# Scaling h by 1/z on VectorE behind the reciprocal, instead of on GpSimd

## The reference

```
h  = x @ W;  f1 = h @ a1;  f2 = h @ a2
e  = leaky_relu(f1 + f2^T, 0.2)
att = softmax(adj * e, axis=1)            # each column of the 2048x2048 scores sums to one
xp = att @ h + bias + x                   # layer 0
y  = adj @ (xp @ W1 + b1)                 # layer 1
y  = relu((y - mean) * rsqrt(var + 1e-5) * gamma + beta)   # statistics over all batches and nodes
out = y + xp
```

## Time and profile before

| | |
|---|---|
| three runs | 1035.03, 1036.02, 1036.68 us; median 1036.02 |
| profiled execution, first to last instruction | 1034.5 us (the runs' times also hold what lies around that: median minus span is 1.5 us) |
| VectorE busy | 937.6 us, 91% |
| TensorE busy | 943.3 us, 91% (ends of matmuls are modelled) |
| ScalarE busy | 771.1 us, 75% |
| GpSimd busy | 553.1 us, 53% |
| batches 1 to 6 | 119.5 to 123.6 us each, from one recip of tile 0 to the next |

### The profile page before, as it was taken

The page is one execution under the profiler, slowest core; times in us unless marked ns, Lnnn a source line. Parts: engine busy times, 40 slices in busy tenths (PEclk is TensorE's granted clock), DMA queues, the critical chain, the costliest instruction groups (busy, mean ns, idle before and its releaser), DMA issues.

```text
span 1034.5 us, 11295 instructions
## 1 busy us (share of the span) xinstructions
PE 943.3 (91%) x2999; PEld 529.0 (51%) x2999; DVE 937.6 (91%) x938; ACT 771.1 (75%) x897; POOL 553.1 (53%) x306
## 2 busy tenths in 40 slices
PE   7998999979999799989999799997999989998980
PEld 5333555555555545546555545555555555554760
DVE  4987899998999699997999959998899979998967
ACT  5877688857887578785878657885788758787646
POOL 1434566664776356673667626665467636666000
PEclk8999999999999999999999999998999999999995
DMA  8955454565456454555445644455545555434978
GB/s 333 421 190 196 177 180 171 202 221 204 173 188 212 168 193 167 224 174 214 165 172 213 219 161 173 173 203 193 204 173 203 211 191 195 175 120 167 355 284 324
DMA packets 45153, 214.14 MB, mean 207 GB/s; under 512 B 5406, under 2 KB 6030, under 8 KB 23438
## 3 DMA queue, kind: packets, MB, share of 16 engines
q1 hardware_dynamic: 45084, 213.32, 56.1%
HBM read 189.07 MB, written 24.23 MB: 206 GB/s over the span
## 4 chain that ended last, share of the span: by engine, by line
issue 35%; DVE 30%; PE 13%; ACT 9%; POOL 7%; DMA 3%; DVEq 2%; ACTq 0%; SPq 0%; POOLq 0%
DVE exp_lo L685 14%; DVE scores L656 7%; DVE scores L666 6%; ACT scores L535 6%; POOL hz L811 3%; PE acc L392 2%; PE acc L430 2%; ACT scores L544 1%; PE acc L457 1%; PE acc L460 1%; PE acc L459 1%; POOL region_even L829 1%; POOL region_odd L829 1%; PE acc L422 1%; DMA f_odd<-biasT 1%
## 5 line engine op out<-in xcount | busy, mean ns | idle before, releaser
L666 DVE CUSTOM_DVE_ANT_0 scores<-scores,adj_slot 128x2048 f32<-128x2048 f32 x128 | 292.1, 2282 | 5.1 <-DVE scores L656 1.8
L544 ACT ACTIVATE scores<-scores,neg_mx 128x2048 f32<-128x2048 f32 x128 | 256.5, 2004 | 4.2
L811 POOL TENSOR_TENSOR hz<-region_even,rz 128x128 f32<-128x128 f32 x64 | 143.4, 2241 | 195.7 <-DVE rz L673 190.0
L811 POOL TENSOR_TENSOR hz<-region_odd,rz 128x128 f32<-128x128 f32 x64 | 140.1, 2190 | 182.5 <-DVE rz L673 178.7
L443 PE MATMUL acc<-adj_slot,region_even 128*128 128x512 f32 x512 | 230.8, 596 | 4.1 <-issue 4.1
L408 PE MATMUL acc<-scores,hz 128*128 128x512 f32 x464 | 209.3, 595 | 12.7 <-POOL hz L811 12.6
L685 DVE TENSOR_TENSOR exp_lo<-scores,exp_hi 128x512 fp32r<-128x512 f32 x280 | 215.6, 827 | 3.8 <-ACT exp_hi L554 3.8
L443 PE MATMUL acc<-adj_slot,region_odd 128*128 128x512 f32 x392 | 175.3, 592 | 0.8 <-DVE region_odd L717 0.8
L656 DVE SCALAR_TENSOR_TENSOR scores<-scores,f,f_even 128x2048 f32<-128x2048 f32 x64 | 156.8, 2450 | 12.3 <-ACT scores L535 12.1
L656 DVE SCALAR_TENSOR_TENSOR scores<-scores,f,f_odd 128x2048 f32<-128x2048 f32 x64 | 157.9, 2467 | 8.6 <-issue 6.5
L422 PE MATMUL acc<-exp_hi,hz_lo 128*128 128x512 f32 x280 | 132.2, 472 | 36.7 <-POOL hz_lo L823 36.1
(11 more groups left out here) (79 smaller groups left out, 847.6 us busy)
## 6 DMA issues: line engine op xcount, KB each, us to landing
adj_slot<-adjT SPq DMA_DIRECT2D x128, 1024.0 KB, 4.8
adj_slot<-xT SPq DMA_DIRECT2D x13, 1024.0 KB, 9.2
adj_slot<-xp_dram SPq DMA_DIRECT2D x8, 1024.0 KB, 7.0
adj_slot<-y_dram SPq DMA_DIRECT2D x7, 1024.0 KB, 7.0
outT<-adj_slot SPq DMA_DIRECT2D x6, 1024.0 KB, 4.7
f_odd<-f_rows SPq DMA_DIRECT2D x4, 1024.0 KB, 6.7
region_even<-xT SPq DMA_DIRECT2D x16, 256.0 KB, 4.9
f_even<-biasT SPq DMA_DIRECT2D x16, 256.0 KB, 4.1
```

Of the source, the lines that this page charges most:

```text
L544: act.activation(scores[e][:, :], scores[e][:, :], ACT.Exp, bias=neg_mx[:, e:e + 1], accum_out=zsum[:, e:e + 1]).then_inc(exp_done, 1)
L666: dve.tensor_tensor_reduce(scores[e][:, :], scores[e][:, :], slots[s][:, :], 1.0, NEG_BIG, ALU.mult, ALU.max, mx[:, e:e + 1]).then_inc(max ...
L811: scaled = pool.tensor_tensor(hz[e][:, :], region[bt.par][:, tile_cols(t)], rz[:, e:e + 1].to_broadcast([P, P]), ALU.mult)
```

## The change

VectorE now runs scale_h(t) directly behind recip(t), for all 128 tiles, with `tensor_scalar` (the scalar is rz) instead of GpSimd's `tensor_tensor` with a broadcast rz. For a split tile the two instructions that made hz and hz_hi on GpSimd become one that makes hz_hi, and hz_lo = h * rz - hz_hi is one `scalar_tensor_tensor`. VectorE gets the waits of scale_h (h_out, the ring, rz_done, split_used, hz_scaled) and loses wait_hz. GpSimd keeps only its four add_bias a batch.

```diff
             def recip(bt, t):
                 e = t % ER
                 dve.wait_ge(exp_done, NT * bt.n + t + 1)
-                wait_hz(bt, t)
                 dve.reciprocal(rz[:, e:e + 1], zsum[:, e:e + 1]).then_inc(rz_done, 1)
+            def scale_h(bt, t):
+                e = t % ER
+                if t % TC == 0:
+                    dve.wait_ge(h_out, NC * bt.n + t // TC + 1)
+                wait_ring(dve, bt, t)
+                dve.wait_ge(rz_done, NT * bt.n + t + 1)
+                if t in WHOLE or is_first(bt):
+                    dve.tensor_scalar(hz[e][:, :], region[bt.par][:, tile_cols(t)], rz[:, e:e + 1], None,
+                                      ALU.mult).then_inc(hz_done, 1)
+                    return
+                m = SPLIT.index(t)
+                dve.wait_ge(split_used, NS * bt.n + NC * (m - 1))
+                dve.tensor_scalar(hz_hi[m % 2][:, :], region[bt.par][:, tile_cols(t)], rz[:, e:e + 1], None,
+                                  ALU.mult).then_inc(hz_scaled, 1)
+                dve.wait_ge(hz_scaled, len(SPLIT) * (bt.n - 1) + m + 1)
+                dve.scalar_tensor_tensor(out=hz_lo[e][:, :], in0=region[bt.par][:, tile_cols(t)], scalar=rz[:, e:e + 1],
+                                         in1=hz_hi[m % 2][:, :].bitcast(F32), op0=ALU.mult, op1=ALU.subtract)\
+                    .then_inc(hz_done, 1)
...
                         recip(bt, t)
+                        scale_h(bt, t)
...
                 if not is_last(bt):
                     recip(nx, 0)
+                    scale_h(nx, 0)
...
         def _(pool):
-            def scale_h(bt, t):
-                e = t % ER
-                pool.wait_ge(rz_done, NT * bt.n + t + 1)
-                if t % TC == 0:
-                    pool.wait_ge(h_out, NC * bt.n + t // TC + 1)
-                wait_ring(pool, bt, t)
-                scaled = pool.tensor_tensor(hz[e][:, :], region[bt.par][:, tile_cols(t)],
-                                            rz[:, e:e + 1].to_broadcast([P, P]), ALU.mult)
-                if t in WHOLE or is_first(bt):
-                    scaled.then_inc(hz_done, 1)
-                    return
-                scaled.then_inc(hz_scaled, 1)
-                m = SPLIT.index(t)
-                pool.wait_ge(split_used, NS * bt.n + NC * (m - 1))
-                pool.tensor_tensor(hz_hi[m % 2][:, :], region[bt.par][:, tile_cols(t)],
-                                   rz[:, e:e + 1].to_broadcast([P, P]), ALU.mult).then_inc(hz_scaled, 1)
-                pool.wait_ge(hz_scaled, 2 * (len(SPLIT) * (bt.n - 1) + m + 1))
-                pool.tensor_tensor(hz_lo[e][:, :], hz[e][:, :], hz_hi[m % 2][:, :].bitcast(F32),
-                                   ALU.subtract).then_inc(hz_done, 1)
...
             def step(bt):
-                for t in range(NT):
-                    scale_h(bt, t)
-                    if t == NT - 2 and not is_first(bt):
-                        add_bias(bt, 0)
-                        add_bias(bt, 1)
-                for c in range(0 if is_first(bt) else 2, NC):
+                for c in range(NC):
                     add_bias(bt, c)
```

More of the change, by code:

```diff
@@ L671, in recip @@
                 dve.wait_ge(exp_done, NT * bt.n + t + 1)
-                wait_hz(bt, t)
                 dve.reciprocal(rz[:, e:e + 1], zsum[:, e:e + 1]).then_inc(rz_done, 1)
-            def wait_hz(bt, t):
-                if not (is_first(bt) and t < ER):
-                    dve.wait_ge(hz_done, NT * bt.n + t - ER + 1)
+            def scale_h(bt, t):
[16 more added lines that the diff above has]
+                    .then_inc(hz_done, 1)
             def exp_low(bt, t):
```

## The result

| | before | after |
|---|---|---|
| median of the runs, us | 1036.35 (1035.03 to 1036.85) | 1062.56 (1059.46 to 1063.69) |
| profiled execution: time, span | 1036.02, 1034.5 | 1059.46, 1057.7 |
| granted TensorE clock, profiled execution | 0.969 | 0.968 |

The changed kernel takes 1.0242 times as long, 95% interval 1.0219 to 1.0264: 26 us slower. The forecast was 3.9 us slower, with a range up to 1057 and a chance of 0.13 for the rival that comes nearest, exposed waits. The profiled execution of after is its fastest; the other three have spans of 1060.0 to 1061.9 at clocks of 0.960 to 0.965, and all that follows is read from spans of profiled executions.

A forecast was written before the change was run, and what follows sets the result against it. VectorE was taken to set the mid-batch pace, with TensorE waiting at batch ends. Stream +12.3, batch 0 +1.5 and ends -9.9 gave +3.9 us on a 1034.5 span: 1038.4, median 1040; range 1024 to 1057.

The forecast's parts named there:

- exposed waits: VectorE's rz_done and hz_scaled waits expose register work, 0.2 us more a split tile, 0.1 a whole one: 1057 us; chance 0.13.
- The port relief: Mid-batch, VectorE's exp_lo and leaky get shorter without GpSimd's products on the shared port: 5.35 us a batch saved.
- 0.034 us: On VectorE, an instruction waiting for its forerunner's semaphore starts this long after the forerunner's end.
- 0.045: Split tiles on VectorE: cost in us of the extra split_used wait before the product, taken from between 0 and 0.15.
- tensor_scalar's 0.23 us: VectorE's new 128x128 product, not in the trace, was priced as the nearest instruction, a copy of 128x128.
- The ends: Six batch ends: support product earlier as TensorE no longer waits for hz_lo; five gain 1.5 us, one 2.4, together 9.9.
- The other ends are like batch 3's: Batch ends other than batch 5's were taken to match batch 3's within 0.15 us, gaining 1.5 us each.
- done with tile 15 at about 469.5: End of batch 3: with hz there, TensorE finishes tile 15 then, before the first xp at 471.65 us.
- Batch 0: Whole tiles alone, 0.14 us each, 2.2 us, partly hidden by waits for the exponential: +1.5 us, between 0 and 3.5.
- TensorE's wait for hz_lo at the ends: Sign at batch ends: TensorE's 3.74 us wait for tile 15's hz_lo would be gone.

The follow-up runs named there:

- products later: Changed kernel, for tiles 1 to 14 the first product placed behind the next score and the second behind the leaky after it; 1025.43 us, 0.9885 of before.
- the run with the small instructions: Changed kernel with ten small VectorE instructions ahead of all other work, five kinds at 128 and 512 columns, each behind its forerunner's semaphore; one execution, 1059.11 us.
- the run with the waits ahead: Changed kernel with the waits on h_out, TensorE's ring and split_used moved before the reciprocal's own; 1050.01 us, 1.0126 of before.
- the kernel before with the adds held: Kernel before the change, GpSimd's adds of batches 1 to 7 waiting until exp_lo of tile 15 is through; 1013.98 us, 0.9788 of before.

## Why the prediction was wrong

**The bound and the direction were right.** VectorE paces the stream and what is added to it is paid in full; the change is slower. The port relief came as priced: with the measured 0.42 us a whole tile, 0.87 a split one behind an exp_low, 0.73 one without (0.95 less 0.22), tiles 0 to 13 add some 9.1 us a batch, and the streams grew by 27.5/7 = 3.9, which leaves 5.2 for the relief (5.35 forecast). The run with GpSimd's products put back prices them at 31.0/7 = 4.4, at other places.

**The step that failed is what a wait costs.** The forecast took "0.034 us" behind a forerunner and "0.045" for split_used, from a gap at the kernel's start where one wait had one direct forerunner. That made a gap behind the reciprocal of 0.034 us in a whole tile and 0.079 in a split one. Measured are 0.11 and 0.19; over the seven streams the gaps sum to 17.2 us instead of 6.2. What was missed is that a wait on another semaphore in front of the product keeps the queue from having the product ready when the reciprocal ends, even if its condition is long true. Moving such waits took 11.0 us out of the streams, of which the forecast held 63 x 0.045 = 2.8: 8.2 us missed. The rival "waits are exposed" had named this mechanism, but got 0.13, because I argued that a few queue instructions would run under the new instructions. They stand under a reciprocal of 0.16 us and not under one of 0.29, and under a whole score or leaky they cost nothing (products later). Nor is the price one number: in batch 7, outside the loop, where the same waits have constant values, seven of the nine split tiles have a gap of 0.09 us instead of 0.19. No run isolates why.

The Trainium skill, "VectorE: DVE Perf Modes", "The DRAIN you can't avoid", has semaphores between chained instructions cost nothing extra. The runs don't agree. Between small instructions with one direct semaphore each the gap is 0.03 us, while a leaky without such a wait starts 0.09 us before the end of the tensor_scalar in front of it (432.25 against 432.34, in the run with the later products); behind a reciprocal, with further waits in between, the gap is 0.11 and 0.19, and the placement of those alone was worth 11.0 us.

**tensor_scalar's 0.23 us was a copy's.** It reads its scalar from a tile, 0.06 us more: 14 tiles x 7 batches x 0.056 = 5.5 us. The row for it was there: leaky and tensor_tensor gave me 0.34 against 0.28 us for the same two-input work with and without such a scalar, and I didn't carry the difference over.

Together 13.7 of the 17.1 us. Another 3.4 are steps of batches 1 to 6 in which VectorE starts an instruction late, at the same places in each pass of the loop: the product of tile 3 in batches 1, 3 and 5 (gap 0.40 us instead of 0.09), that of tile 8 in batches 2, 4 and 6 (0.49 instead of 0.14), the step of tile 10 in the odd ones (0.11 longer), and the first leaky behind tile 0's product in the even ones (a gap of 0.30). Tile 8 of batch 2, first in after and then in the run with the small instructions, where the gap is 0.14:
```profile
300.40 0.29 DVE L682 TENSOR_SCALAR hz<-region_even,rz 128x128 f32<-128x128 f32 x1 [0.49 <-DVE rz L672]
...
299.47 0.15 DVE L673 RECIPROCAL rz<-zsum 128x1 f32<-128x1 f32 x1
299.76 0.29 DVE L683 TENSOR_SCALAR hz<-region_even,rz 128x128 f32<-128x128 f32 x1
```
TensorE's ring is not the cause, although one of the six is put down to it (0.51 us, `acc`): the wait asks for tile 4, and TensorE is at tile 7's products by then in both traces. In the run with the small instructions (one execution), whose loop is the same, all these delays are gone and the streams take 698.5 us; in the two runs that changed only GpSimd's adds they are where they were. With the waits ahead, three of 0.35 us a step stand in front of tile 3's reciprocal instead. So they go with VectorE's own program and where the instructions stand in it; what makes them no run shows. About 1.3 of the 3.4 are in the 11.0 already, since the run with the waits ahead was rid of 2.3 and got 1.1 new ones. scalar_tensor_tensor took 0.35 us instead of 0.34, 0.7 in all. The last 0.6 us stay open.

**The ends: the right sum from the wrong order, and one end taken for all.** In batch 3 the first exp_lo chunk was forecast at 466.2, 8.5 us behind tile 14's reciprocal, and came 8.49 behind it (478.21 - 469.72); the end gained 1.30 us against 1.23 forecast in these terms. But add 0 did not follow the reciprocal: nothing precedes it on GpSimd, so it asked for the port during the score and got it before leaky, 3.35 us. "The other ends are like batch 3's" failed: they gained 0.18 to 1.93 us, although VectorE's rows up to the end of exp_lo are alike to 0.02 us. The difference between them is TensorE's clock behind its idle 4.4 us. Stretches of the span with each engine's busy time; the granted clock is the third number from the end (0.54, 0.68). First about the time of the twelve products at batch 1's end, then at batch 3's:
```profile
228.00:233.00 5.00, 5.00 (x15) 3.89 (x15) 5.00 (x10) 1.67 (x1) 1.29 (x1) 0.54 0.74 262
479.00:483.30 4.30, 4.30 (x14) 3.46 (x15) 4.30 (x8) 2.00 (x2) 1.29 (x1) 0.68 0.77 274
```
In batch 1 nearly all of them run at the lower level, 1.2 GHz, 0.43 us apart; the second pair is from the upper one, 2.4 GHz, 0.23 apart:
```profile
228.63 0.63 PE L424 MATMUL acc<-exp_lo,hz_hi 128*128 128x512 f32 x1
229.05 0.63 PE L422 MATMUL acc<-exp_hi,hz_lo 128*128 128x512 f32 x1
...
482.20 0.39 PE L424 MATMUL acc<-exp_lo,hz_hi 128*128 128x512 f32 x1
482.43 0.39 PE L422 MATMUL acc<-exp_hi,hz_lo 128*128 128x512 f32 x1
```
Up to the start of the next product they take 5.16 us (227.61 to 232.77) and 4.17 (478.94 to 483.11), where the kernel before with the adds held takes 2.84 (456.09 to 458.93) at a clock of 1.00; the support product starts 15.27 and 14.28 us behind tile 14's reciprocal. So TensorE was not "done with tile 15 at about 469.5", and it is late again, by the clock. The same goes for the 3 us that the ends gave less than forecast: they are no more than two traces of this kernel differ by (144.7 and 148.4), with VectorE's rows up to exp_lo alike. That the median of the runs lies 3 us above the profiled execution may be of this kind too; the clocks of the other executions (0.960 to 0.965) fit it, no trace of them shows it.

**Batch 0** cost 0.7 + 0.6 us in its two parts, 1.5 forecast. TensorE's wait for hz_lo at the ends is gone by name only: in its place it waits 4.4 us for exp_lo at each of the six, 26.5 of the 67.2 us that it waits for exp_lo in the whole span.

## What to carry to other kernels

Price a new instruction on a busy engine with all that stands in front of it in the queue: a wait whose condition is long true is free under a long instruction and costs 0.06 to 0.16 us behind a short one on whose result it depends. Put such an instruction one long instruction behind its producer; here that turned 27.5 us lost into 3.8 won. And before crediting an idle stretch to the engine named as its releaser, look at what stands ahead in that engine's queue: holding four adds back took 24 us off the span of the kernel before without moving a product.

## What the runs showed of the hardware

- An add of 128x512 on GpSimd, two SBUF inputs, beside VectorE's back-to-back instructions costs these 0.7 to 1.1 us each, up to three in a row, and shifts from victim to victim: leaky 2.35 to 3.35, tensor_scalar 0.29 to 0.95 or 1.39, scalar_tensor_tensor 0.35 to 1.25, four exp_lo chunks 2.49 to 3.55 us.
- A per-partition scalar from a tile costs VectorE 0.06 us, whatever the width (0.29 against 0.23 us at 128 columns, 0.49 against 0.43 at 512).
- After 4.4 us of idle TensorE, the granted clock was 0.54 over the products that followed in one batch and 0.68 in another, at starts that lay alike to 0.02 us; that spread is worth 1 us an end.
- Waits on VectorE's queue whose conditions had long been true left a gap of 0.11 us behind a 0.16 us reciprocal in whole tiles, 0.19 in split ones inside the loop and 0.09 in most of them outside it; with only the direct wait it was 0.04.
- Some instructions of VectorE's loop start 0.3 to 0.4 us late in every pass, at places that stayed when GpSimd's adds were moved and changed with VectorE's own program. The cause is open.
